# Softmax maxima and scores: four and two PSUM banks in place of three and three, two maxima to an instruction

## What is computed

```python
# x, ctx: (8, 256, 512); 16 heads of 16 channels; 512 positions
q = Wq @ layernorm(x) + bq;  k = Wk @ ctx + bk;  v = Wv @ ctx + bv
scores = einsum('bhkt,bhks->bhts', q, k) / sqrt(16)
p = softmax(scores, axis=-1)
x = x + Wo @ einsum('bhts,bhks->bhkt', p, v) + bo
x = x + ffn(layernorm(x))     # RMS norm, router, top 2 of 8 experts, shared expert
```

## Time and profile before

| what | value |
|---|---|
| median of 3 runs | 982.48 us (976.42 to 984.2) |
| the profiled execution | 983.02 us |
| its span, first to last instruction | 981.2 us, mean granted clock 0.908 |
| before stage 0's first score | 0 to 86 us |
| stages 0 to 15 | 86 to 596 us |
| feed-forward layer | 597 to 981 us |

### The profile page before, as it was taken

One profiled execution on the slowest core, in us unless ns is written; L12 is line 12 of the kernel. 1 busy time (PEld: TensorE's weight loads), 2 busy tenths in 40 slices (PEclk: granted clock), 3 DMA queues, 4 the chain that ended last, 5 costly groups with the idle time before them and its releaser, 6 DMA issues. The chain is left out here.

```text
span 981.2 us, 10867 instructions
## 1 busy us (share of the span) xinstructions
PE 887.3 (90%) x3648; PEld 378.8 (39%) x3648; DVE 478.5 (49%) x915; ACT 408.3 (42%) x753; POOL 222.2 (23%) x204
## 2 busy tenths in 40 slices
PE   6669999899898999989998998896999999999993
PEld 3233333233333333333332224662444444444441
DVE  3587777577576776777786006557221111111110
ACT  1003676556566566666677543220002223222320
POOL 3100212402223114131100003000012444444431
PEclk9655999899899999999998557977999999999997
DMA  6772456636435546356431014910352454544552
GB/s 221 191 173 98 111 132 140 127 81 144 111 98 130 136 112 135 93 137 145 102 80 24 15 34 149 399 43 1 127 201 57 87 89 87 101 89 86 92 91 32
DMA packets 46788, 110.44 MB, mean 113 GB/s; under 512 B 11648, under 2 KB 12672, under 8 KB 42432
## 3 DMA queue, kind: packets, MB, share of 16 engines
q1 hardware_dynamic: 35376, 80.26, 32.1%
q0 software_dynamic: 11328, 29.37, 14.8%
q10 hardware_dynamic: 32, 0.13, 0.0%
HBM read 68.44 MB, written 41.16 MB: 112 GB/s over the span
## 5 line engine op out<-in xcount | busy, mean ns | idle before, releaser
L663 DVE TENSOR_REDUCE negmax<-smax_ps 128x1 f32<-128x512 f32 x512 | 325.3, 683 | 133.4 <-PE smax_ps L558 132.2
L488 ACT ACTIVATE probs<-st_ps 128x512 f32<-128x512 f32 x512 | 273.7, 603 | 156.5 <-PE st_ps L584 156.4
L584 PE MATMUL st_ps<-q_stack,k_stack 50*128 50x512 f32 x512 | 163.9, 522 | 21.0 <-ACT probs L488 21.0
L558 PE MATMUL smax_ps<-k_stack,q_stack 48*128 48x512 f32 x512 | 143.6, 455 | 14.0 <-DVE negmax L663 7.3
L597 PE MATMUL pv_ps<-probs,v_t 128*32 128x512 f32 x1024 | 148.5, 654 | 3.5 <-ACT probs L488 1.7
L1087 PE MATMUL big_ps<-w_gu,attn 128*128 x312 | 140.5, 593 | 0.8 <-ACT attn L928 0.8
L584 PEld LDWEIGHTS st_ps<-q_stack,k_stack 50*128 50x128 f32 x512 | 63.1, 197 | 178.6 <-ACT probs L488 118.2
L892 POOL DMA_INDIRECT out<-x_sb,row_i x39 | 61.7, 1582 | 140.2 <-ACT x_sb L935 127.0
L558 PEld LDWEIGHTS smax_ps<-k_stack,q_stack 48*128 48x128 f32 x512 | 67.8, 200 | 38.9 <-DVE negmax L663 26.3
L1273 DVE TENSOR_TENSOR zeros<-attn,big_ps 128x256 f32<-128x256 f32 x39 | 16.4, 421 | 135.0 <-ACT attn L947 135.0
L1087 PEld LDWEIGHTS big_ps<-w_gu,attn 128*128 128x128 f32 x312 | 56.2, 190 | 57.0 <-issue 57.0
(11 more groups left out here) (150 smaller groups left out, 676.5 us busy)
## 6 DMA issues: line engine op xcount, KB each, us to landing
parts_dram<-parts SPq DMA_DIRECT2D x32, 512.0 KB, 6.0
k_stack<-parts_dram SPq DMA_DIRECT2D x32, 256.0 KB, 4.5
q_stack<-parts_dram SPq DMA_DIRECT2D x32, 256.0 KB, 5.1
w_gu<-in_gate_up SPq DMA_DIRECT2D x8, 1024.0 KB, 14.7
x_sb<-in_x SPq DMA_DIRECT2D x8, 512.0 KB, 7.1
c_sb<-in_ctx POOLq DMA_DIRECT2D x8, 512.0 KB, 5.2
k_stack<-parts_dram SPq DMA_DIRECT2D x32, 128.0 KB, 5.0
q_stack<-parts_dram SPq DMA_DIRECT2D x32, 128.0 KB, 5.7
```

The source lines that it names most:

```text
L488: nc.scalar.activation(probs[:, k % 2, u % GH, :], score_bank(UNITS * s + u), ACT.Exp, scale=SCALE).then_inc(exp_done, 1)
L558: nc.tensor.matmul(smax_bank(i), q_stack[buf][low:low + SROWS, pair, tt * P:(tt + 1) * P], k_stack[buf][low:low + SROWS, pair, :], start=T ...
L584: nc.tensor.matmul(score_bank(i), k_stack[buf][low:end, pair, st * P:(st + 1) * P], q_stack[buf][low:end, pair, :], start=True, stop=True, ...
L663: nc.vector.tensor_reduce(negmax[:, n % 2, c:c + 1], smax_bank(UNITS * n + u), AX_X, ALU.max, negate=True).then_inc(max_done, 1)
```

## The change

MAXBUF goes from 3 to 4 and STBUF from 3 to 2; the eight banks are still all used. `maxima` is called for every second unit only, waits for both passes of the pair, and takes both maxima in one instruction from two neighbouring banks (128 partitions x 2 x 512 elements) into two columns of `negmax`, 16 apart; it adds 2 to max_done. The casts that stood behind units 5 and 13 before stage 0 stand behind 4 and 12. `max_pass`, `scores` and the order of TensorE's and ScalarE's work are as before but for the two constants.

```diff
-MAXBUF = 3
-STBUF = 3
+MAXBUF = 4
+STBUF = 2
...
                 def maxima(n, u):
-                    dve.wait_ge(s_ready, UNITS * n + u + 1)
+                    dve.wait_ge(s_ready, UNITS * n + u + TILES)
                     if u == 0 and n >= 2:
                         dve.wait_ge(nm_turned, n - 1)
-                    c = u % TILES * (UNITS // TILES) + u // TILES
-                    nc.vector.tensor_reduce(negmax[:, n % 2, c:c + 1], smax_bank(UNITS * n + u),
-                                            AX_X, ALU.max, negate=True).then_inc(max_done, 1)
+                    c, bank = u // TILES, (UNITS * n + u) % MAXBUF
+                    nc.vector.tensor_reduce(negmax[:, n % 2, c:c + UNITS // TILES + 1:UNITS // TILES],
+                                            smax_ps[:, bank:bank + TILES, :], AX_X, ALU.max, negate=True).then_inc(max_done, TILES)
...
-                for u in range(UNITS):
+                for u in range(0, UNITS, TILES):
                     maxima(0, u)
-                    if u in (5, 13):
-                        high(2, u // 13)
+                    if u in (4, 12):
+                        high(2, u // 12)
...
-                for u in range(LEAD):
+                for u in range(0, LEAD, TILES):
                     maxima(1, u)
...
-                        if n < HALVES:
+                        if n < HALVES and u % TILES == 0:
                             maxima(n, (u + LEAD) % UNITS)
```

## The result

Before, the median is 983.3 us (four runs, 976.4 to 990.2); after, it is 1,053.2 us (four runs, 1,040.4 to 1,056.2). The ratio is 1.063, 95% interval 1.048 to 1.079: slower, as forecast, by 62 us where 44 were forecast, and inside the range of 1,010 to 1,048. The mean granted clock is 0.867 for 0.908.

What follows compares the result with a forecast made beforehand. TensorE was taken as attention's pace-setter, stopping for ScalarE's bank. In us, 48.8 - 15 + 3.9 + 7.3 - 1.5 = 43.5 on 983.0 gave 1,026.5, range 1,010 to 1,048.

Steps and rivals of the forecast that it cites:

- the ring: Attention, score banks three to two: each score waits for exponential u-2, not u-3; 48.8 us in stages 0 to 12.
- The second score at T+1.68: Four-unit step without projections, T its start: next pair's second score moves from T+1.18, waiting for the second exponential, 0.50 later.
- the working for 20 to 24: Units 20 to 24 of a stage: score 23 waits for exponential 21 behind V's copy; pv 0.72 us later.
- A plain step: Four units of attention without projections: 2.93 us grows to 3.43, 0.50 more.
- A tail without and a head: Stage's units 14 to 0 without output projection cost 2.67 us more, units 0 to 12 cost 1.13 more.
- What is given back: Odd stages' first projection: longer tails cover five waits for the context and the half clock behind; 15 us returned.
- Stages 13 to 15: End of attention: plain steps, steps with the pv copy and half-clock steps lose 3.9 and 7.3 us.
- Pairs and the fourth bank: Before stage 0, where VectorE bounds: paired maxima at 1.13 us against 1.20 for two, and more lead; -1.5 us.
- rival 1: Clock falls in the thinned steps: 3.1 us a tail, 1,067 for all 13, 1,045 for a few; chance 0.14.
- A ring that costs plain steps only: Attention: TensorE and ScalarE catch up outside steps without projections; +2 us, so 985; chance 0.07.
- two banks that suffice: Score ring: no slowdown, only the pairs' gain is left, 981.5 us, or 978 at the bound; chance 0.05.
- an overhead of VectorE: Maxima throughout: 256 pairs each save 0.07 to 0.12 us, 18 to 31 in all, 952 to 965; chance 0.03.

Runs made afterwards that it cites:

- experiment 2: Four maximum banks and two score banks, single maxima, against the kernel before: 1,048.9 us, ratio 1.061.
- experiment 1: Two score banks alone, three maximum banks with single maxima, against the kernel before: 1,049.4 us, ratio 1.064.
- experiment 9: Kernel before plus 256-column matmuls of zeros behind every second pair of scores in stages 14 and 15: 968.4 us, ratio 0.984.
- experiment 10: Changed kernel, maximum passes between a pair's scores at some places, plus 256-column zero matmuls behind each pair in stages 14 and 15: 1,007.1 us.
- experiment 7: Kernel before plus 256-column matmuls of zeros behind each pair of scores from unit 8 of stage 14: 968.2 us, ratio 0.986.

## Why the forecast was half right

The time lies inside the range, but the sum behind it does not hold term by term: the ring was taken some 7.5 us too large, and the clock, which cost some 26 us in the runs compared and 34 in the profiled one, at nothing. That 1,045.4 is inside owes something to luck.

**The ring.** Right in place and mechanism, too large in size. The second score at T+1.68 is there to 0.01 us; score 23 goes 1.24 us behind score 22, as the working for 20 to 24 has it (0.75 of wait in the row at 146.80 above). The mis-sized term is what follows the second score: I kept the distance to pv at 0.76, and it is 0.65, since the two maximum passes between take 0.72 us for 0.82. Why they are shorter isn't shown. A plain step thus costs 0.39 for 0.50. A tail without and a head with no fall cost 3.2 us together for 3.80, a tail with output 3.3 for 3.68. Over everything the ring cost about 36 us for 43.5.

**What is given back.** Right: no wait for the context is left, and the 15.3 us that stood over 28.93 in five intervals are all inside the +23.8 measured.

**Stages 13 to 15.** Without further falls the intervals to the turn in stage 14 cost 6.7 us (3.8 and 2.9), and the stretch behind it 4.5; forecast for all of it were 13.9 (3.9, 7.3 and stage 12's tail of 2.67). A step at half clock takes 4.55 us for 4.06, against 4.58 forecast.

**Pairs and the fourth bank.** Right to a microsecond: 1.13 us a pair in the stream, 1.23 for a lone one (1.21 forecast), and -0.5 at stage 0's first score for -1.5 forecast; in this trace the bank was no help (experiment 2 leaves it open for single maxima). Elsewhere nothing that the times show, as said.

**The clock.** This step failed. I gave it 0.14, because "their idle time grows in bits of 0.5 us, while each drop seen within a stage followed over 2 us of standing". The trace before did not bear that out. It has a drop within stage 14 behind a wait of 1.10 us:

```profile
531.30 0.79 PE L584 MATMUL st_ps<-q_stack,k_stack 50*128 50x512 f32 x1 [1.10 <-ACT probs L488]
```

In the changed kernel five tails of 13 fell behind waits of at most 0.75 us, more than the two that I named as the point from which the rival decides: rival 1, at 0.14, is what happened. The price was too low as well: 3.1 us a fall, taken from the interval from 161.91 to 196.25 beside its long wait, for 5.05 measured; and where no projections follow, as from stage 12 on, one fall cost 9.1 and 4.8 us in two intervals. The rival's own figure for a few falls, 1,045, is the measured one by two errors that cancel, too large a ring and too low a price. The place could have been read: the plain steps of the earlier trace rows were at full clock, but the end of stage 14 in the earlier trace rows showed that steps with little between their waits can stay at half clock for long, and the tail around u = 22 was where I had added most, 0.72 and 0.75. The Trainium skill (TensorE: Matmul & The Clock Gate, A second HAM failure mode: psum-queue depth-cycling) describes such a clock for another kernel, one that oscillates on the small idles of a ring of PSUM banks; the trace after agrees, at 5.05 us a fall.

**The other rivals.** A ring that costs plain steps only (985), two banks that suffice (981.5) and an overhead of VectorE (952 to 965) are all out: experiment 1 has the whole loss with VectorE's part untouched.

## What to carry to other kernels

A bank taken from a ring cost here one release of its consumer per group of four, less what then ran side by side (0.50 less 0.11 us), and could be read from one step: who goes late, by how much, and what runs beside it then. Price the clock apart from that: list the places where the added waits of TensorE stand close together, and take the cost of a fall from steps of the same kernel at either level. And before giving a ring its bank back, look at the order: needed work put into the wait returned some 40 of 62 us here, while the same order with three maximum banks waited for VectorE instead.

## What the hardware did that I had not expected

The granted clock fell from 1.00 to 0.50 in tails in which TensorE's longest wait was 0.75 us, in five of the eight without an output projection (stages 0 to 12), in the changed kernel as in experiments 1 and 2. They were those of stages 1, 2, 4, 8 and 12 twice and of 1, 2, 4, 6 and 10 once, with the same instructions in each tail but for the maxima's form. In experiment 9 the clock fell within stage 14, between 531.1 and 532.2, with no wait of TensorE over 0.31 us in the 15 us before. What decides it in a given tail stays open.

Low clock lasted under load: TensorE was busy 37.7 of 40 us at a granted clock of 0.52 in the changed kernel, and in experiment 10 full clock returned 30 us after the first filling (554.4 to 584.2), 24 of them without a wait; in experiment 7, with the same 256 columns behind each pair, it returned 3 us after the first (530.0 to 533.0).

Matmuls of zeros that nobody reads made the kernel before 1.6% faster (experiment 9, interval 1.1 to 2.1%), because 2.68 us a step at full clock, with its filling, is less than 4.06 at half clock without.
